# Two-layer model with routed experts on one core: sums of weighted activations split once for two three-pass products

## The reference

```python
base1 = t @ w1.T
base3 = t @ w3.T
h1 = base1[None] + SCALING * jnp.einsum('etr,efr->etf', jnp.einsum('td,erd->etr', t, a1), b1)
h3 = base3[None] + SCALING * jnp.einsum('etr,efr->etf', jnp.einsum('td,erd->etr', t, a3), b3)
act = jax.nn.silu(h1) * h3
out_e = jnp.einsum('etf,df->etd', act, w2) + SCALING * jnp.einsum('etr,edr->etd', jnp.einsum('etf,erf->etr', act, a2), b2)
out = jnp.einsum('te,etd->td', weights, out_e)
```

## Time and profile before

| What | Value |
|---|---|
| Median of 3 runs | 1060.06 us (1056.37 to 1061.72) |
| The profiled execution | 1054.69 us, its span 1053.0 us |
| TensorE busy | 980.6 us (93%), weight loads 669.9 us |
| VectorE busy | 711.2 us (68%) |
| ScalarE busy | 507.9 us (48%) |
| GpSimd busy | 500.1 us (47%) |

### The profile page before, as it was taken

How to read it: one execution, slowest core, us unless ns; L and a number is a source line. 1 busy time by engine, 2 the same in 40 slices (tenths; PEclk the granted TensorE clock), 3 DMA queues, 4 the chain that set the end, 5 groups by cost and what they waited for, 6 DMA issues and landing times. The chain is left out here.

```text
span 1053.0 us, 15574 instructions
## 1 busy us (share of the span) xinstructions
PE 980.6 (93%) x4429; PEld 669.9 (64%) x4429; DVE 711.2 (68%) x2140; ACT 507.9 (48%) x1039; POOL 500.1 (47%) x485
## 2 busy tenths in 40 slices
PE   3999999999999999999999999899988999889993
PEld 2766667656565665656566656477864667648873
DVE  5787779788786877879797776445543667634542
ACT  3433454655646556564453332144534777515451
POOL 3456555554535545354654655524451155423443
PEclk9999999999999999999999999999999999989997
DMA  6069000000000000000000002146534000015651
GB/s 181 1 284 415 3 1 1 1 1 1 1 0 2 0 1 1 1 0 1 12 3 9 11 11 71 39 137 197 166 94 140 1 22 22 22 42 178 194 174 34
DMA packets 42900, 65.12 MB, mean 62 GB/s; under 512 B 7153, under 2 KB 25121, under 8 KB 40640
## 3 DMA queue, kind: packets, MB, share of 16 engines
q1 hardware_dynamic: 37824, 55.59, 16.1%
q0 software_dynamic: 4992, 8.54, 2.4%
HBM read 37.20 MB, written 28.74 MB: 63 GB/s over the span
## 5 line engine op out<-in xcount | busy, mean ns | idle before, releaser
L362 PE MATMUL bank<-split 128*128 128x512 f32 x416 | 206.9, 497 | 7.8 <-DVE ud L1267 4.1
L364 PE MATMUL bank<-split 128*128 128x512 f32 x416 | 165.2, 397 | 0.0
L363 PE MATMUL bank<-split 128*128 128x512 f32 x416 | 164.8, 396 | 0.0
L863 ACT ACTIVATE sil<-bank 128x512 f32<-128x512 f32 x128 | 76.2, 595 | 116.0 <-PE bank L364 115.2
L1644 POOL TENSOR_TENSOR gsum<-act 128x512 f32<-128x512 f32 x64 | 84.9, 1327 | 81.5 <-DVE act L1203 81.4
L421 PE MATMUL bank<-act,a 128*128 128x512 f32 x256 | 117.6, 592 | 0.0
L362 PEld LDWEIGHTS bank<-split 128*128 128x128 f32 x416 | 79.5, 191 | 48.8 <-issue 17.4
L1199 DVE TENSOR_TENSOR act<-bank,sil 128x512 f32<-128x512 f32 x128 | 87.8, 686 | 17.2 <-PE bank L364 14.2
L363 PEld LDWEIGHTS bank<-split 128*128 128x128 f32 x416 | 79.9, 192 | 28.3 <-issue 18.6
L688 PE MATMUL bank<-xlT,e 128*128 128x256 f32 x368 | 91.2, 392 | 5.1 <-ACT xlT L1068 2.7
L1203 DVE TENSOR_TENSOR act<-act,wT 128x512 f32<-128x512 f32 x128 | 91.7, 716 | 4.4
(11 more groups left out here) (283 smaller groups left out, 1957.6 us busy)
## 6 DMA issues: line engine op xcount, KB each, us to landing
e<-e_dram SPq DMA_DIRECT2D x92, 256.0 KB, 3.1
rows_in<-yw SPq DMA_DIRECT2D x17, 1056.0 KB, 17.8
xin<-rows_in SPq DMA_DIRECT2D x46, 132.0 KB, 3.0
x<-rows_out SPq DMA_DIRECT2D x8, 256.0 KB, 4.7
rows_in<-yw,slot_i POOLq DMA_INDIRECT x64, 2.3
rows_out<-ob,ids POOLq DMA_INDIRECT x46, 2.3
out<-ob,ids POOLq DMA_INDIRECT x46, 2.4
act<-b_dram SPq DMA_DIRECT2D x2, 256.0 KB, 3.1
```

Of the source, the lines that this page charges most:

```text
L362: mm(dst, w[0], m[0], start=start, stop=False, **more)
L363: mm(dst, w[0], m[1], start=False, stop=False, **more)
L364: return mm(dst, w[1], m[0], start=False, stop=stop, **more)
L863: af(sil[(k - 1) % 2][:, :], bank[BH1[STEPS[k - 1][0] % 2]][:, :], ACT.Silu).then_inc(silu_done.sem, 1)
```

## The change

All four sums are kept, each written over expert 1's block in `act1[j]`. ScalarE takes the high part of each (`sums_high`), GpSimd the low part (`sums_low`), and these two parts serve two three-pass products: `w2` times the sum (`down`), and `a2` times the sum (`value_sum`), which replaces `a2` times expert 1's blocks. Expert 0's values remain, in three passes for blocks 0 and 1 (`values_high`, `values_low`), in full for blocks 2 and 3. The masks are rearranged accordingly: the sum's value times mask 1, minus expert 0's value times the difference of the masks. The fourth `down` moves from the end of the slot into the next slot. `w2` and `a2` are split once, in slot 0. To find room, some buffers share memory (`iv` with `gi`, `oaT` with `go`, the first mask has one buffer), and the weights of the second layer are loaded only after the last feed-forward chunk. The order on TensorE, ScalarE and GpSimd changes with that.

```diff
+            gs = [(part(35 + j), part(j)) for j in range(J)]
+            vs = [(part(43 + j), part(J + j)) for j in range(2)]
...
                 if call == 0:
                     sp.wait_ge(*h3_ready(MAINS - 1))
+                    for dst, src in late_loads:
+                        sp.dma_start(dst, src).then_inc(late_loaded.sem, 16)
...
                     for j in js:
-                        pe.wait_ge(*weighted(n, STEP[j, e]))
-                        last = mm(bank[BV][:, :], a2[:, j, :], act_[e][j][:, :], start=j == 0, stop=j == J - 1)
+                        if j < len(vs):
...
+                            pe.wait_ge(*value_low(g, j + 1))
+                            last = mm3(bank[BV][:, :], tuple(w[:, rows(j)] for w in a2s), vs[j], j == 0, False)
+                        else:
+                            pe.wait_ge(*weighted(g, STEP[j, 0]))
+                            last = mm(bank[BV][:, :], a2[:, j, :], act0[j][:, :], start=False, stop=j == J - 1)
...
+                def value_sum():
+                    if l is None:
+                        return
+                    pe.wait_ge(*r_done(l, 1))
+                    pe.wait_ge(*sum_low(l))
...
+                    for j in range(J):
+                        last = mm3(bank[BV][:, :], tuple(w[:, rows(j)] for w in a2s), gs[j], j == 0, j == J - 1)
+                    last.then_inc(v_ready.sem, 1)
+
+                def down(n, j):
...
+                    pe.wait_ge(*sum_low(n, j + 1))
+                    mm3(bank[BOUT][:, :], tuple(w[:, rows(j)] for w in w2s), gs[j], j == 0, False)
...
                 a_den()
+                down(l, 3)
                 h(3, 2)
                 pre_T()
                 a_back()
-                value(1, range(J))
+                value_sum()
...
-                down(2)
+                down(g, 2)
                 a_gate(2)
-                down(3)
                 a_gate(3)
...
+                def values_high(j):
+                    if g is None:
+                        return
+                    act.wait_ge(*weighted(g, STEP[j, 0]))
+                    act.wait_ge(*v_ready(g - 1, 1))
+                    af(vs[j][0], act0[j][:, :], ACT.Copy).then_inc(value_high.sem, 1)
+
+                def sums_high(j):
+                    if g is None:
+                        return
+                    act.wait_ge(*summed(g, j + 1))
+                    act.wait_ge(*v_ready(g - 1))
+                    af(gs[j][0], act1[j][:, :], ACT.Copy).then_inc(sum_high.sem, 1)
...
                 out_T()
+                values_high(0)
+                values_high(1)
                 silu(5)
+                sums_high(0)
                 a_mid_T()
...
                 silu(6)
+                sums_high(1)
                 a_mid(0)
...
                 silu(8)
+                sums_high(2)
                 up_high(0)
...
                 up_high(1)
+                sums_high(3)
                 a_norm(1)
...
                     pool.wait_ge(*weighted(g, STEP[j, 1]))
-                    pool.wait_ge(*w2_used(g, j - 1))
-                    pool.tensor_tensor(out=gsum[j % 2][:, :], in0=act_[0][j][:, :], in1=act_[1][j][:, :], op=ALU.add).then_inc(summed.sem, 1)
+                    pool.tensor_tensor(out=act1[j][:, :], in0=act0[j][:, :], in1=act1[j][:, :], op=ALU.add).then_inc(summed.sem, 1)
+
+                def sums_low(j):
+                    if g is None:
+                        return
+                    pool.wait_ge(*sum_high(g, j + 1))
+                    pool.tensor_tensor(out=gs[j][1], in0=act1[j][:, :], in1=gs[j][0].bitcast(F32), op=ALU.subtract).then_inc(sum_low.sem, 1)
+
+                def values_low(j):
+                    if g is None:
+                        return
+                    pool.wait_ge(*value_high(g, j + 1))
+                    pool.wait_ge(*summed(g, j + 1))
+                    pool.tensor_tensor(out=vs[j][1], in0=act0[j][:, :], in1=vs[j][0].bitcast(F32), op=ALU.subtract).then_inc(value_low.sem, 1)
...
                 total(1)
+                sum_weights_low()
+                sums_low(0)
                 f_scale()
+                sums_low(1)
                 mask_diff()
+                values_low(0)
                 a_scale()
+                values_low(1)
                 r_scale(s.r_stat)
                 total(2)
+                sums_low(2)
+                up_low(0)
                 total(3)
-                up_low(0)
                 up_low(1)
+                sums_low(3)
                 a_product()
                 r_scatter(s.r_sort)
```

More of the change, by code:

```diff
@@ L155, in build, with part, parts @@
         rf = sb("rf", [P, T])
+        rows_in = nc.dram_tensor("rows_in", [NROWS, W], F32, kind="Internal").ap()
+        rows_out = nc.dram_tensor("rows_out", [NCH * S, P], F32, kind="Internal").ap()
+        stats_l = sb("stats_l", [P, T, 6]); part_l = sb("part_l", [P, 4, T])
+        mv_l = [sb(f"mv_l{i}", [P, T]) for i in range(2)]; sc_l = [sb(f"sc_l{i}", [P, 2, T]) for i in range(2)]
+        yn_l = [yn_f, yn_a]
+        vu = [z, h2]
+        nb_l = sb("nb_l", [P, T]); nmx = sb("nmx", [P, 2]); rs = sb("rs", [P, 2]); rsi = sb("rsi", [P, T])
+        with nc.sbuf_tensor("split", [P, 45 * S], F32R) as split:
+            def part(n):
+                return split[:, n * S:(n + 1) * S]
+            def parts(n):
+                return part(n), part(n + 1)
+            gs = [(part(35 + j), part(j)) for j in range(J)]
+            vs = [(part(43 + j), part(J + j)) for j in range(2)]
+            w1s, w3s, b1s, b3s = (parts(6 + 2 * i) for i in range(4))
+            a1s, a3s = (tuple(split[:, 14 * S + (k + i) * P:14 * S + (k + i + 1) * P] for k in range(2)) for i in (0, 2))
+            ts = [parts(15), parts(17)]
+            uas = [[parts(19 + 8 * p + 2 * i) for i in range(2)] for p in range(2)]
+            uds = [[parts(23 + 8 * p + 2 * i) for i in range(2)] for p in range(2)]
+            w2s, a2s = parts(39), parts(41)
+        act1 = [sb(f"act1{j}", [P, S]) for j in range(J)]
+        act0 = [sb(f"act0{j}", [P, S]) for j in range(2)] + act0_high
+        act_ = [act0, act1]
+        w1, w3, b1, b3 = act0
+        yT, zT, pr_, pT = [tT, hT], mT1, act0[0:2], act0[2:4]
+        a1, a3 = act1[0][:, 0:P], act1[0][:, P:2 * P]
+        wk_l1 = sb("wk_l1", [P, P]); wq_l1 = sb("wq_l1", [P, P]); wv_l1 = sb("wv_l1", [P, P])
+        waT = sb("waT", [P, P]); wbT = sb("wbT", [P, P])
+        wak = sb("wak", [P, P]); gmat = sb("gmat", [P, P]); wuT = sb("wuT", [P, P])
         cnt = sb("cnt", [P, E]); cnt_i = sb("cnt_i", [P, E], I32); nt_i = sb("nt_i", [P, E], I32); ntf = sb("ntf", [P, E])
@@ L407, in h, with value @@
                         mm3(b[:, :], cut(lora), uds[p][i], False, True, skip_group_check=True).then_inc(ready.sem, 1)
-                def value(e, js):
-                    n = g if e == 0 else l
-                    if n is None:
+                def value(js):
+                    if g is None:
                         return
-                    if e == 0 and js[0] == 0:
+                    if js[0] == 0:
                         pe.wait_ge(*r_done(g - 1))
@@ L666, in first_layer @@
                 h(3, 8)
-                value(0, (0, 1))
+                value((0, 1))
                 a_gate(0)
@@ L1649, in values @@
                     pool.wait_ge(*r_done(l))
[L1650 removed]
+                    pool.tensor_tensor(out=r1[:, :], in0=r2[:, :], in1=r1[:, :], op=ALU.subtract).then_inc(r_ready.sem, 1)
                 def f_scale():
```

126 lines of the change are left out of this document (62 added, 64 removed).

## The result

The changed kernel takes 1134.65 us (median of 4 runs, 1132.62 to 1135.77), the kernel before in the same session 1059.44 (1056.37 to 1061.72): a ratio of 1.071, 95% interval 1.068 to 1.074. It is slower, as forecast, but by 75 us and not by 35, and outside the range (1062 to 1126).

What follows compares the result with a forecast made beforehand. TensorE was taken as the bound (busy 517.6 of 524 us), with GpSimd's second half of a slot deciding. Terms 19.2 + 6.0 + 2.3 + 4.4 + 1.0 + 2.0 = 34.9 us gave 1095 against the median of 1060.06; range 1062 to 1126.

Steps and rivals of the forecast that it cites:

- the chain in slot 7: Second mask, value's low part, sum 2, ScalarE's copy, up parts, gi: gate product 2.5 us late, 2.4 a slot net.
- At nothing: Items priced at zero: seven late loads, the gates' in-place buffers and the single first mask add no wait.
- TensorE's empty time: Idle time in the slots was to rise about 64 us: 28.8 less work and 34.9 longer.
- slots 13 and 14: VectorE is late there anyway, so the walk costs only 0.5 us each, 1.0 in all.
- slots 3 to 10: Slots with gates: the gate chain is 2.4 us late in each of eight slots, 19.2 us.
- the walk: Step-by-step timing of a slot's GpSimd and ScalarE work from the second mask on, 1.22 us per GpSimd subtraction.
- Is done before it: Slot 7, GpSimd: sum 1's low part, queued behind sc_f (313.0), is done before the mask is saved at 314.05.
- surprise: TensorE waiting at the w2 products for the first or second sum's low part, which was not expected.
- rival 2: Collisions on the shared path come on top and VectorE gets late itself: 25 us more, 1120; chance 0.22.
- collisions: GpSimd and VectorE on their shared port pair: 14 us in 15 slots, about 25 with VectorE's side, outside the sum.
- The first: Rival: TensorE stays the bound, GpSimd and ScalarE have more slack, 28.8 us are saved, 1031; chance 0.10.
- The third: Rival: chain and gain cancel, about half the predicted lateness, 1060; chance 0.06.

Runs made afterwards that it cites:

- e15: Changed kernel with no sums or values split, and the fourth w2 product and total(3) back in their old places: 1058.2 us.
- e11: Changed kernel with nothing split, but ScalarE's six high-part copies a slot made and read by nobody: 1075.3 us.
- e5: Changed kernel plus products of a zero weight tile on TensorE ahead of two waits in each feed-forward slot but the first: 1136.0 us.
- e13: Changed kernel with each of GpSimd's six subtractions a slot replaced by three memsets, the third cut to half to match the length: 1123.8 us.
- e10: Changed kernel with nothing of the sums or values split, all products of a2 and w2 in full precision: 1079.5 us.
- e6: Changed kernel with memsets in place of GpSimd's six subtractions a slot, before their length was matched: 1131.2 us.
- e18: Whole changed kernel with total(3) back ahead of up_low(0) on GpSimd: 1134.4 us.
- e12: Changed kernel with all copies and subtractions, but its ten three-pass products a slot each made as one full-precision product: 1142.0 us.
- e1: Changed kernel with both low parts of expert 0's values moved ahead of f_scale on GpSimd: 1127.2 us.
- e3: Changed kernel with the values' low parts early, and sum 2's copy and low part behind the first up projection's high and low parts: 1140.2 us.

## Why the prediction was right and wrong

**Right: direction, place, and the chain in slot 7.** Slot 7 went the way it was walked: GpSimd between the second mask and sum 2, ScalarE's copy waiting "about 3 us in a slot" (3.34), gi late. "At nothing" held for late loads and the gates' shared buffers (e15), and the copies were free (e11). What TensorE would wait for went less well: gi was to stand first, and stands behind both kinds of new low part and VectorE, with 9.6 us. GpSimd's busy time rose by 136 us, forecast 120.

**Right by luck: TensorE's empty time.** It was to rise by 64 us and rose by 68.5. But the forecast paired that with 28.8 us less work, and the work grew by 4.8. The 33.6 us between are about what 59 us at half clock hold (half of them, 30). In e5, at a fuller clock, this is waiting and not gain: with the zero products left out, TensorE is without work for 70.7 + 27.9 = 98.6 us there, so an estimate of the time without work is near 100 us, where the prediction's own would be 64 + 10.2. The prediction did not think of the clock at all.

**Wrong: the terms of the sum, by a factor of 1.7 to 2.5, and of seven in slots 13 and 14.** From one copy of oT to the next, after against before (slot 0: up to the first copy):

| term | priced | measured |
|---|---|---|
| slots 3 to 10 | 19.2 | 38.2 (3.7 to 6.4 each) |
| slots 1 and 2 | 6.0 | 10.2 |
| slot 0 | 2.3 | 5.2 |
| slots 11 and 12 | 4.4 | 7.5 |
| slots 13 and 14 | 1.0 | 7.3 |
| the end | 2.0 | 4.9 |
| sum | 34.9 | 73.3 |

The step that failed is the walk's assumption that a queue's lateness begins at the second mask, with the first half hiding what lies there and VectorE on time, and that each operation lasts its pitch of 1.22. What stood in its place:
- In slot 7 itself the walk is 1.2 us short at the second value's low part: 17.4 us behind the slot's copy of oT (338.25 here, 302.60 in the kernel before), walked 16.2. "Is done before it" failed: the low part of sum 1 ends at 350.05, the mask is saved at 349.58, and the mask difference starts at 350.01. Then the attention's scale waits 0.64 for VectorE, where the walk had GpSimd back to back.
- The first half did not hide the early low parts. In slots 1, 2 and 3 TensorE waits 1.85 us each for a sum's low part, in slot 4 3.09, 19.1 us in 11 waits over the run: the "surprise" of the prediction's last part.
- A sum's low part lasted 1.48 us on the mean, a value's 1.31; undisturbed it is 1.26.
- Slots 13 and 14 were priced 0.5 each, since VectorE was late there anyway. Being late already, it passed every collision on: 4.12 us of wait instead of 1.56. VectorE's ud released 17.0 us of TensorE's waits (4.1 before), in slots 9 to 14, the mark set for rival 2.
- The 14 to 25 us of collisions were kept outside the sum. Their share of the kernel's time is some 11 us for VectorE's side (e13), and more by what they lengthen GpSimd's queue, which no run separates; that they exist should have been in it, with the sign that was certain. The Trainium skill (SBUF — State Buffer, Who interferes with whom) says that a VectorE instruction with two SBUF inputs contends with a GpSimd instruction that reads SBUF, and not with one that only writes it. e10 and e15 agree (0.69 against 1.39 and 1.76), and so do memsets for subtractions: VectorE's busy time goes from 571.2 back to 510.5 (e6).
- One move inside the frame, total(3) behind up_low(0), was read as part of the order and given no price of its own. In the frame without splits it is 26 us; in the whole change it is nothing (e18), so it is no part of what the sum missed.

**Rivals.** The second, collisions and VectorE late on top of the chain (1120, chance 0.22), is nearest to what came, by its marks and its time; still 15 us short, and what it does to VectorE carries 11. The first fell: e12 finds 7.4 of 28.8 us left. The third, 1060, is excluded by the time.

What stays open: the runs give the six subtractions 66 us, of which about 11 is collision on VectorE's side; how the other 55 divide among the chains (gates, values, w2 products, next slot's start) is not settled, since e1 to e3 and e18 show that mending one hands the time to the next.

## What to carry to other kernels

An engine busy 98% of the time is not evidence that the others have slack: here the gate chain through the three others already held it up, by 0.38 us in slot 7, and cheaper work for the bound gave 7 us of 29 while 96 small steps elsewhere cost 66. Before work is moved off the bound, ask of each place where the new steps stand who waits for the queue behind them, and price them at the mean of such steps beside a busy neighbour. When the cost doesn't yield, strip the change to its frame: here the frame alone hid a swap of two steps worth 26 us, which only a kernel with nothing else in it could show. Then try the piece in the whole change before counting on it: there the same swap was worth nothing.

## What the runs showed of the hardware

Behind waits such as the 2.44 us of slot 7 TensorE's granted clock went from 2.4 to 1.2 GHz for 3.4 us (6.8 in some places), in a kernel in which TensorE is busy 89% of the stretch; a pass then takes 0.63 us instead of 0.39. With 27 us of low clock in the slots' stretch instead of 59, bought with 27.9 us of zero products, the time was as it was (e5).

A memset on GpSimd of 128x512 takes 0.53 us. With memsets in the subtractions' places VectorE's weightings last 727 ns on the mean (e6) and 747 (e13), with subtractions 787 and up to 1.83 us, in the kernel before 716; the median is 692 or 693 in all of these. The mean depends on where the other steps stand too: e10 has 785 without any new low part, and e15, two edits away, 720.
